# Cross-attention stack on one Trainium2 core: another order of the last scores and half output products in the first masked phase

## What is computed

```python
# grouped
q = (rmsnorm(x) * norm_w) @ wq; k = cond @ wk; v = cond @ wv      # 16 heads over 4 kv heads
x = x + softmax(q k^T / sqrt(32)) v @ wo
# masked
q = x @ Wq; k = ctx @ Wk; v = ctx @ Wv                            # 16 heads of 64
x = x + softmax(q k^T / 8 + col_bias) v @ Wo + bo
```

## Time and profile before

| what | value |
|---|---|
| median of 3 runs | 1507.51 us (1506.37 to 1511.48) |
| the profiled execution | 1509.95 us, span 1508.2 us |
| TensorE busy | 1487.8 us, 99% of the span |
| VectorE, GpSimd, ScalarE busy | 989.6, 912.7, 744.5 us |
| chain that ended last | PE 87%, POOL 4%, DVE 3%, ACT 2% |

### The profile page before, as it was taken

One profiled execution on the slowest core, in us unless ns is written; L12 is line 12 of the kernel. 1 busy time (PEld: TensorE's weight loads), 2 busy tenths in 40 slices (PEclk: granted clock), 3 DMA queues, 4 the chain that ended last, 5 costly groups with the idle time before them and its releaser, 6 DMA issues.

```text
span 1508.2 us, 23315 instructions
## 1 busy us (share of the span) xinstructions
PE 1487.8 (99%) x8480; PEld 1232.5 (82%) x8480; DVE 989.6 (66%) x1644; ACT 744.5 (49%) x1317; POOL 912.7 (61%) x825
## 2 busy tenths in 40 slices
PE   7998999999999999999999999999999999999998
PEld 7987887888778887888788877888788877887787
DVE  5676757765776657665776667565766577666764
ACT  4566576335733564346633573346533663357321
POOL 0074467557765587567756686468756775568541
PEclk9999999999999999999999999999999999999999
DMA  9999562122312231132212232143113231222101
GB/s 323 327 405 409 199 232 91 42 79 84 126 52 69 98 119 50 44 126 83 79 46 76 92 112 64 34 136 119 43 43 103 81 101 53 65 99 91 57 1 56
DMA packets 101649, 170.12 MB, mean 113 GB/s; under 512 B 17056, under 2 KB 51360, under 8 KB 95520
## 3 DMA queue, kind: packets, MB, share of 16 engines
q1 hardware_dynamic: 97552, 151.06, 30.3%
q10 hardware_dynamic: 3824, 17.04, 2.8%
q0 software_dynamic: 160, 0.53, 0.1%
HBM read 116.95 MB, written 51.65 MB: 112 GB/s over the span
## 4 chain that ended last, share of the span: by engine, by line
PE 87%; POOL 4%; DVE 3%; ACT 2%; SPq 1%; DMA 1%; issue 1%; ACTq 0%; DVEq 0%
PE OB L375 16%; PE OB L376 15%; PE OB L377 15%; PE SB L375 10%; PE SB L377 9%; PE SB L376 9%; POOL xhl L1344 4%; PE TB L507 3%; PE MX L507 3%; PE TB L543 1%; PE SB L484 1%; DMA s_fm<-prob 1%; PE OB L430 1%; PE OB L427 1%; ACT xhl L851 1%
## 5 line engine op out<-in xcount | busy, mean ns | idle before, releaser
L1315 POOL TENSOR_TENSOR prob<-prob,small 128x512 f32<-128x512 f32 x256 | 278.7, 1091 | 255.3 <-DVE small L1115 255.0
L816 ACT ACTIVATE prob<-prob 128x512 f32<-128x512 f32 x128 | 80.8, 632 | 274.2 <-DVE prob L1102 271.6
L1093 DVE SCALAR_TENSOR_TENSOR prob<-SB,aux 128x512 f32<-128x512 f32 x128 | 88.0, 688 | 182.4 <-PE SB L377 181.8
L1309 POOL TENSOR_TENSOR prob<-prob,small 128x512 f32<-128x512 f32 x128 | 136.2, 1064 | 117.3 <-DVE small L1087 117.0
L375 PE MATMUL SB<-foldM,xhl 128*128 128x512 f32 x512 | 203.9, 398 | 1.6 <-issue 0.3
L375 PE MATMUL OB<-pT,foldN 128*128 128x512 f32 x512 | 205.0, 400 | 0.0
L376 PE MATMUL OB<-pT,foldN 128*128 128x512 f32 x512 | 199.8, 390 | 0.0
L377 PE MATMUL SB<-foldM,xhl 128*128 128x512 f32 x512 | 199.7, 390 | 0.0
L377 PE MATMUL OB<-pT,foldN 128*128 128x512 f32 x512 | 199.7, 390 | 0.0
L376 PE MATMUL SB<-foldM,xhl 128*128 128x512 f32 x512 | 199.4, 389 | 0.0
L1087 DVE TENSOR_REDUCE small<-prob 128x8 f32<-128x512 f32 x128 | 87.1, 680 | 93.0 <-ACT prob L826 91.6
(11 more groups left out here) (140 smaller groups left out, 3851.4 us busy)
## 6 DMA issues: line engine op xcount, KB each, us to landing
prob<-in_wkvM_dram SPq DMA_DIRECT2D x32, 512.0 KB, 8.4
ring<-s_fm SPq DMA_DIRECT2D x64, 256.0 KB, 5.5
ring<-s_fn SPq DMA_DIRECT2D x128, 128.0 KB, 2.6
out_dram<-x ACTq DMA_DIRECT2D x15, 1024.0 KB, 3.9
s_fm<-prob SPq DMA_DIRECT2D x16, 512.0 KB, 8.4
wraw<-in_wqG_dram SPq DMA_DIRECT2D x8, 1024.0 KB, 6.8
s_fn<-x SPq DMA_DIRECT2D x16, 512.0 KB, 5.8
ring<-in_xT_dram SPq DMA_DIRECT2D x32, 256.0 KB, 3.2
```

Source lines behind the costliest of these rows:

```text
L816: act.activation(own, own, ACT.Exp).then_inc(S["exped"], 1)
L1093: dve.scalar_tensor_tensor(out=own, in0=bank, scalar=M_SCALE, in1=row, op0=ALU.mult, op1=ALU.add).then_inc(S["biased"], 1)
L1309: pool.tensor_tensor(own, own, hmax[u % 2].unsqueeze(2).broadcast_to([P, HH, KEYS]), ALU.subtract).then_inc(S["evac"], 1)
L1315: pool.tensor_tensor(own, own, rsum[u % 2].unsqueeze(2).broadcast_to([P, HH, KEYS]), ALU.mult).then_inc(S["normed"], 1)
```

## The change

In phase 2, once a pass, two half output products come earlier on TensorE: half (2, 0) is moved from behind score 5 to behind score 4, and half (3, 0) from behind the first transpose to behind score 5. Each of the last four scores is then followed by one half. Nothing else is changed, on TensorE or elsewhere.

```diff
@@ -666,13 +666,13 @@
                 out_part(it, 2, 1, 1)
                 mixing(it, 2, 1)
                 scores(it, 2, 4, first)
+                out_part(it, 2, 2, 0)
                 scores(it, 2, 5, first)
-                out_part(it, 2, 2, 0)
+                out_part(it, 2, 3, 0)
                 scores(it, 2, 6, first)
                 out_part(it, 2, 2, 1)
                 scores(it, 2, 7, first)
                 transposes(it, 3, 0, first)
-                out_part(it, 2, 3, 0)
                 out_part(it, 2, 3, 1)
```

## The result

The changed kernel took 1520.28 us (median of 5 runs, 1518.41 to 1521.01) against 1507.23 us for the kernel before (1506.37 to 1511.48). The ratio is 1.0079, 95% interval 1.0066 to 1.0092: slower by 0.8%. Its profiled execution took 1520.46 us.

What follows compares the result with a forecast made beforehand. TensorE was taken to bound the kernel, busy 1487.8 of 1508.2 us, with a chain of waits leaving it at score 7's end. One half product, 1.36 us, over eight passes adds 10.9 us to 1507.51: 1518.4 us, range 1513.5 to 1524.

Steps and rivals of the forecast that it cites:

- The place: TensorE ahead of product 0: a new gap of some 1.3 us once a pass, released by VectorE's update or low part.
- The size: Score 7 ends one half product later: 1.36 us a pass, 10.9 us over eight passes, giving 1518.4 us.
- The covers at zero: Moved halves on TensorE find operands ready, and VectorE is ready when score 7 ends: price 0.
- The update of chunk 0 worth 0: Banks 0 and 1 finish earlier, but VectorE's written order keeps the X update behind later work: worth 0.
- Contention: GpSimd's work against the chain behind score 7, such as VectorE's shift: taken as zero, ends 6.9 and 18.2 us.
- The hit shift of the rival: GpSimd's norm of unit 5 slows VectorE's shift of unit 7 by up to 0.91 us: 1525.7 us, chance 0.06.
- The clock: Rival: the new TensorE gap lowers its granted clock, 1.3 us more a pass, 1528.8 us; chance 0.05.
- the one stretch named: TensorE's 3.5 us from 142.8, granted clock 0.64, behind a 1.75 us gap; the clock was called full otherwise.
- Hidden slack: Rival: cover behind score 7 on TensorE has slack the chain doesn't show; price 0, 1507.5 us; chance 0.09.
- the two small waits: TensorE waits in the kernel before: 0.12 us ahead of product 0, about 0.34 at score 0's second chunk.

Runs made afterwards that it cites:

- e2: Kernel before with only half (3,0) moved, to directly behind half (2,0), which stays behind score 5; ratio 1.0068 to the kernel before.
- e5: Changed kernel with half (3,1) also moved ahead of score 7, so four halves stand ahead of it; ratio 1.0170 to the kernel before.
- e1: Kernel before with only half (2,0) moved, from behind score 5 to behind score 4; ratio 1.0012 to the kernel before.
- e3: Changed kernel with half (2,1) moved from ahead of score 7 to behind the first transpose; ratio 1.0020 to the kernel before.
- e9: Kernel before with half (2,1) moved ahead of score 6, so score 6 is late and score 7 in its old place; ratio 1.0018.
- e4: Kernel before with half (2,1) moved from ahead of score 7 to behind the first transpose; ratio 0.9973 to the kernel before.
- e8: Kernel before with halves (2,0) and (2,1) moved behind the first transpose, none between scores 4 to 7; ratio 0.9962.
- e7: Changed kernel with VectorE updating X chunks 0 and 1 before taking score 7, ScalarE's order left alone; ratio 1.0041 to the kernel before.
- e6: Changed kernel with VectorE updating X chunks 0 and 1 before taking score 7 and ScalarE rounding them before unit 7's exponential; ratio 1.0105.

## Why the prediction was right, point by point

**The place**, right: the loss is one new gap a pass, ahead of product 0, released by VectorE's update (1.25 us where "some 1.3 us" was said), in all eight passes. With VectorE's order as written, the kernels that hold score 7 back (changed, e2, e5) have it in full, 1.25 or 2.65 us; those that keep it in place (e1, e3, e9) have 0.33 us of it, from VectorE's lateness, and those that advance it (e4, e8) have none.

**The size**, right: 1.36 us a pass was predicted, 1.41 measured; 10.9 us predicted, 11.9 us by the ratio (9.9 to 13.9), 13.1 us by the two medians, and 1518.4 us against 1520.28 us, in the range of 1513.5 to 1524. Of the 0.05 us a pass I know no cause.

**The covers at zero**: both moved halves found their operands ready, no new wait stands ahead of them. VectorE was ready for score 7, with 0.77 us of idle time instead of the 0.4 us worked out, since its shift of unit 6 took 1.03 us, not 1.40. The statement was right for this change alone; e1, e3 and e9 show that the term is not zero once two scores follow each other without a half between them.

**The update of chunk 0 worth 0**, right, and shown by e7 to hang on the written order.

**Contention**: zero was taken, and the shift of unit 7 took 0.69 us. The reason given, that every neighbour moves by the same 1.36 us, was not quite so: the faster shift of unit 6 brought the norm of unit 5 forward, and the distance to the shift grew from 0.73 to 1.09 us. The hit shift of the rival didn't happen here; it did in e6, at 1.68 us where the bound was 1.60.

**The clock**: didn't fall at the gaps of 1.25 us in the changed kernel, nor at those of 0.88 us in e7. But the rival was nearer than 0.05 made it look: at gaps of 1.87 us, 0.6 us more, it fell in four of seven. And one sentence was wrong: the clock of the kernel before was not full outside the one stretch named. Its trace has another low stretch:

```profile
16.50:20.00 3.50, 3.50 (x21) 3.50 (x22) 0.74 (x3) 1.86 (x3) 0.19 (x1) 0.64 0.90 257
```

The page's digits hide it, since a 9 stands for 90% or more.

**Hidden slack**: none. e4 found 0.44 us a pass to be had by giving cover back, which is the size of the two small waits, so these were real waits and not an effect of the modelled ends.

## What to carry to other kernels

When the chain of waits leaves the bounding engine and comes back later, the work that this engine has left behind the point of departure is cover, and moving a piece of it ahead of that point costs its whole length once the cover is just used up; moving one the other way gains only the small wait that is there. A score that leaves earlier helps only as far as the engine that takes it is ready, so count both ends: the arrival of the last unit, and the arrival of each earlier unit plus the taker's time per unit. An early result is worth nothing while its reader has it behind later work in a written order, and what an edit frees on one engine may collide with the path on another.

## What the runs showed of the hardware

Of the gaps of this phase, the granted clock fell at those of 1.87 us (e6, four of seven) and 2.65 us (e5, three of eight), to about 0.6 over stretches of 3.5 us; single microseconds inside them show 0.50, the lower of its two levels, 1.2 in place of 2.4 GHz. It did not fall at gaps of 1.25 us (changed and e2, eight each) or less. Mostly TensorE was working again when the clock fell; at one gap of e5 it fell while the engine still stood, 1284.20 to 1284.60 us at 0.50 with product 0 at 1284.62. The length alone doesn't decide: gaps of one length in one kernel had a fall in some passes and not in others, and the 1.75 us gap of the earlier trace rows, which stands in all eleven traces, has one behind it in seven of them and none in e5, e7, e8 and e9. One fall cost 1.0 to 1.3 us in e5; in e6 a pass with one took 168.2 us (product 0 to product 0, 447.09 to 615.26) and one without 166.55 us (615.26 to 781.81), 1.65 us. The Trainium skill (TensorE: Matmul & The Clock Gate, section "Why this matters for your kernels") advises to keep idle gaps out from between bursts of matmuls, as they bring the lower clock back, but only gaps longer than any of these. e5 and e6 agree that gaps bring it back; but here gaps of 1.87 us already did, so on the length the page and the measurement differ, and the measurement decides.

A shift of VectorE (two inputs, 128 x 512) took 0.69 us with GpSimd idle, and 1.03 to 1.68 us where it began behind a GpSimd operation that was still running. It ended some 0.55 us behind the end of that operation in each case looked at (before: 434.08 and 433.54 us; changed: 439.47 and 438.93 us), so most of its own 0.69 us came on top of the wait.
